# A four-layer graph network on one core: score rows of the last stage by one transpose, a store and a broadcast load, in place of eight transposes and two powers

## The chip, the cores and the metric

One core of one Trainium2 chip. The time is the device time of one execution in microseconds; a lower one is better. The profile is one further execution, taken by the hardware profiler.

## The reference

`x` is (16, 1024, 128), `adj` a 0/1 matrix (16, 1024, 1024). Four layers, each with a layer norm and a relu ahead of it and added to `x`. Layer 0 is a mean over neighbours with two batch norms. The others are attentions over each of the 16 graphs:

```python
# layer 1 ("A"); layer 3 ("C") is the same with adj > 0, other weights, and an elu on its result
Wh = h @ W.T
s, t = Wh @ a_src, Wh @ a_dst
e = leaky_relu(s[:, :, None] + t[:, None, :], 0.2)
alpha = softmax(where(adj == 0, -inf, e), axis=-1)
x = x + alpha @ Wh
# layer 2 ("B")
e = leaky_relu(einsum('bid,bjd,d->bij', h, h, a_0), 0.2)      # only adj == 1 occurs besides 0
x = x + softmax(where(adj == 1, e, -9e15), -1) @ h
```

For A and C the kernel splits the exponential: exp(leaky(s + t)) is, up to factors for a row or a column, the larger of a power of s (a row) and a power of t (a value for each partition). So a weight tile is `max(row_e, least) * mask`.

## The kernel before

Stage one (to about 285 us) reads `adj`, makes the masks and layer 0's means; stage two (to about 450 us) does layer 0's second product. The change is in the last stage, which runs from there to the end.

The last stage does layers A, B and C for all 16 graphs as one pipeline. In round `i` graph `i` is in A's product, graph `i - 1` in B, graph `i - 2` in C, and A's weights of graph `i + 1` are prepared. `run(i)` on each engine writes out its order by hand; nothing but semaphores joins the queues. `b` is a graph, `j` a tile of 128 rows of the adjacency (8 of them), `c` a tile of 128 results.

- **TensorE** (`run`, L1333): eight Gram tiles of B (`gram`, L1304, four matmuls of 512 columns and two halves each), between them C's turned input, values, highest score and rows; then A's product (`weigh`, L1319, eight times 8 tiles, the matmuls at L1329), then B's product and between its tiles A's preparation for the next graph (turned input, `values`, `highest`, `rows`), then C's product. A result tile `c` lies in one of two pairs of PSUM banks, changed every two tiles (`take(free_q, ...)`), so tile `c` waits until ScalarE has taken tiles `c - 4` and `c - 3` (for C's tile 2: B's last two tiles).
- **The rows** (`rows`, L1277): `us` holds 1,024 scores as 8 columns of 128 partitions. Each column is broadcast to 128x128 and transposed, four to a call, so that all 128 partitions of a PSUM bank (`LAST`) hold 512 scores. `row_power` (L1104) on ScalarE makes the power of each half into `row_e` (128x1024). Each half waits for the other through the one bank.
- **VectorE** (`run`, L924): the weight tiles of A and C (`weights`, L877, operation at L884) read `row_e`, `least` and a mask tile from a ring of four; B's leaky relu (`leaky`, L889); the norms' statistics; the reciprocal sums of each pair of result tiles (`shares`, L897, operations at L901 and L903), for which ScalarE then scales the pair (`scaled`, L1130, operation at L1141); `split_g`, `split_ag` and `complement` (L894), for which the next Gram product waits. In `run` the order around the A rows is: `weights("A", i + 1, 0)`, `lowest`, `weights("A", i + 1, 1)`, then `shares("B", i - 1, 3)`.
- **ScalarE** (`run`, L1153): copies of the Gram tiles, B's exponentials, norms, powers, scaled results.
- **SP** (L761) issues all loads and stores of the stage in order, each behind the semaphore that frees its buffer: an output, two mask pairs of A, two halves of `off` (B's mask), `qT`, mask pairs of C, `xA`, more masks.
- **GpSimd** makes only the powers for the norms (L819).

The first weight tile of a graph waits for both halves of the row:

```python
if j == 0:
    dve.wait_ge(S[x, "exp"], b + 1)
    dve.wait_ge(S[x, "s_row"], 2 * b + 2)
```

## Time and profile before

| | |
|---|---|
| median of 3 runs | 1610.05 us (1607.6 to 1613.08) |
| the profiled execution: its time, its span | 1606.74 us, 1604.9 us |
| TensorE busy | 1465.7 us, 91% |
| VectorE busy | 1137.0 us, 71% |
| ScalarE busy | 921.2 us, 57% |
| GpSimd busy | 203.2 us, 13% |
| score transposes (L1283) in the trace | 256 |
| DMA | 161.94 MB, 101 GB/s over the span |

Shares of busy time are averages over three stages with different limits. The rows further down are of the last stage; a row of the order of time gives the start from the span's start, the duration, engine, line, operation, what it writes and reads, how many alike stand together, and in brackets for how long the engine sat idle before it and for whom. Matmuls overlap: the distance between two starts says what one costs, not its own duration.

### The profile page before, as it was taken

To read this page: it belongs to the slowest core of one execution; us is meant where nothing else is said; L and a number is where in the kernel's file an instruction comes from. 1 tells how busy PE (TensorE), PEld (TensorE's weight loads), DVE (VectorE), ACT (ScalarE), POOL (GpSimd) and SP (SyncE) were. 2 spreads that over 40 slices of the span, in tenths; PEclk is the share of its full clock that TensorE was granted. 3 is DMA by queue.
4 is the path that set the end of the run, shared out by engine and by line. 5 is a ranking of instruction groups with operands and counts; after the bars stand their busy time and mean duration, and the time that the engine had idled before them with its cause. 6 is when DMAs were issued, how large, how long until landed. Compare 5 with 4: busy or idle time off the path is not lost. (4 is left out here: it accounts for less than half of the span.)

```text
span 1604.9 us, 32666 instructions
## 1 busy us (share of the span) xinstructions
PE 1465.7 (91%) x12740; PEld 1268.5 (79%) x12740; DVE 1137.0 (71%) x3198; ACT 921.2 (57%) x1825; POOL 203.2 (13%) x201
## 2 busy tenths in 40 slices
PE   3999998799836979999999999999999999999984
PEld 2999997555425859899898898988989889898774
DVE  3666664688635577887878878878788787886653
ACT  2777876122224666766657667566675766755620
POOL 4434430000000001011010111100111101010000
PEclk9999999799957989999999999999999999999996
DMA  9999991377811212213222132231322313212010
GB/s 189 207 209 213 210 210 67 110 244 244 288 39 47 79 47 69 76 47 99 54 85 81 39 106 76 57 93 28 112 74 54 93 35 105 67 34 61 28 35 25
DMA packets 108446, 161.94 MB, mean 101 GB/s; under 512 B 9344, under 2 KB 59136, under 8 KB 106240
## 3 DMA queue, kind: packets, MB, share of 16 engines
q1 hardware_dynamic: 85248, 117.86, 24.4%
q0 software_dynamic: 18432, 33.56, 11.4%
q10 hardware_dynamic: 4608, 8.39, 1.5%
q8 instruction: 102, 1.67, 0.4%
q14 instruction: 56, 0.46, 0.1%
HBM read 151.40 MB, written 41.94 MB: 120 GB/s over the span
## 5 line engine op out<-in xcount | busy, mean ns | idle before, releaser
L1329 PE MATMUL ps<-hV,wts_B 128*128 128x129 f32 x2048 | 246.2, 276 | 3.2 <-ACT wts_B L1128 3.0
L1329 PE MATMUL ps<-hP_A,wts_A 128*128 128x129 f32 x2048 | 239.0, 277 | 6.1 <-DVE wts_A L884 3.4
L1329 PE MATMUL ps<-hP_C,wts_C 128*128 128x129 f32 x2048 | 239.1, 277 | 6.0 <-DVE wts_C L884 6.0
L1329 PEld LDWEIGHTS ps<-hV,wts_B 128*128 128x128 f32 x2048 | 238.2, 192 | 4.6 <-ACT wts_B L1128 4.3
L1329 PEld LDWEIGHTS ps<-hP_A,wts_A 128*128 128x128 f32 x2048 | 234.4, 193 | 8.6 <-DVE wts_A L884 5.2
L1329 PEld LDWEIGHTS ps<-hP_C,wts_C 128*128 128x128 f32 x2048 | 234.3, 193 | 8.3 <-DVE wts_C L884 5.7
L889 DVE SCALAR_TENSOR_TENSOR wts_B<-wts_B 128x1024 f32<-128x1024 f32 x128 | 153.9, 1221 | 30.2 <-ACT wts_B L1124 30.2
L884 DVE SCALAR_TENSOR_TENSOR wts_A<-row_A,least_A,ring_A 128x1024 f32<-128x1024 f32 x128 | 161.2, 1275 | 9.2 <-ACT row_A L1108 8.3
L1124 ACT COPY wts_B<-ps 128x1024 f32<-128x1024 f32 x128 | 129.4, 1011 | 60.0 <-PE ps L1316 60.0
L884 DVE SCALAR_TENSOR_TENSOR wts_C<-row_C,least_C,ring_C 128x1024 f32<-128x1024 f32 x128 | 162.3, 1274 | 0.8 <-DMA ring_C<-maskT_scratch 0.8
L307 ACT ACTIVATE maskT<-ps 128x1024 fp8e4<-128x1024 bf16 x128 | 131.1, 1024 | 49.7 <-PE ps L341 37.7
L1128 ACT ACTIVATE wts_B<-wts_B,shiftB 128x1024 f32<-128x1024 f32 x128 | 141.9, 1153 | 0.0
L353 PE MATMUL ps<-x,adj_b 128*128 128x129 f16 x896 | 120.4, 223 | 18.4 <-DVE x L243 9.4
L354 PE MATMUL ps<-x,adj_b 128*128 128x128 f16 x896 | 120.7, 222 | 0.0
L1313 PE MATMUL ps<-g_hi,ag_hi 128*128 128x512 f16 x256 | 98.1, 383 | 14.7 <-DVE off L894 14.7
L353 PEld LDWEIGHTS ps<-x,adj_b 128*128 128x128 bf16 x896 | 88.2, 99 | 21.3 <-ACT whn L290 11.5
L1141 ACT ACTIVATE quo<-ps,rec_C 128x128 f32<-128x128 f32 x128 | 40.0, 363 | 112.9 <-DVE rec_C L903 112.9
L675 PE MATMUL ps<-maskT,row_hi 128*128 128x512 fp8e4 x256 | 97.3, 380 | 1.2 <-DVE row_lo L593 1.2
L1314 PE MATMUL ps<-g_lo,ag_hi 128*128 128x512 f16 x256 | 98.1, 383 | 0.0
L1315 PE MATMUL ps<-g_hi,ag_lo 128*128 128x512 f16 x256 | 98.1, 383 | 0.0
L1316 PE MATMUL ps<-off,pen_id 128*128 128x512 fp8e4 x256 | 97.9, 382 | 0.0
L675 PE MATMUL ps<-maskT,row_lo 128*128 128x512 fp8e4 x256 | 97.0, 379 | 0.0
(228 smaller groups left out, 2543.2 us busy)
## 6 DMA issues: line engine op xcount, KB each, us to landing
adj_b<-in_adj POOLq DMA_DIRECT2D x128, 256.0 KB, 9.1
maskT_scratch<-maskT SPq DMA_DIRECT2D x16, 1024.0 KB, 6.9
ring_A<-maskT_scratch SPq DMA_DIRECT2D x64, 256.0 KB, 3.3
off<-maskT_scratch SPq DMA_DIRECT2D x32, 512.0 KB, 6.7
ring_C<-maskT_scratch SPq DMA_DIRECT2D x64, 256.0 KB, 3.1
xa<-in_x SPq DMA_DIRECT2D x16, 512.0 KB, 4.3
whT_scratch<-whT_s ACTq DMA_DIRECT2D x32, 256.0 KB, 6.5
whT_b<-whT_scratch SPq DMA_DIRECT2D x16, 512.0 KB, 4.8
```

The source lines that it names most:

```text
L307: nc.scalar.activation(edges[:, b, c, :], psT[c % 2], ACT.Square, scale=EDGE_VALUE ** 0.5, saturate=False, accum_out=sq_all[:, n:n + 1]).t ...
L353: nc.tensor.matmul(q[:, 0:GW], adj_rc, h1, start=(r == 0), stop=False)
L354: nc.tensor.matmul(q[:, 0:P], adj_rc, h2, start=False, stop=False)
L675: last = nc.tensor.matmul(psP[par][:, c * HALF:(c + 1) * HALF], part[:, par, t, :], edges[:, b, t, c * HALF:(c + 1) * HALF], start=(t == 0 ...
L884: nc.vector.scalar_tensor_tensor(wts[x][:, j, :], row_e[x][:, :], least[x][:, j:j + 1], ring[x][:, j % MR, :], ALU.max, ALU.mult).then_inc ...
L889: nc.vector.scalar_tensor_tensor(wts["B"][:, j, :], wts["B"][:, j, :], SLOPE, wts["B"][:, j, :], ALU.mult, ALU.max).then_inc(S["B", "lrelu ...
L1124: nc.scalar.copy(wts["B"][:, j, :], P_SLOTS[j % 2]).then_inc(S["B", "kept"], 1)
L1128: nc.scalar.activation(wts["B"][:, j, :], wts["B"][:, j, :], ACT.Exp, bias=shiftB[:, 0:1]).then_inc(S["B", "exps"], 1)
L1313: nc.tensor.matmul(P_SLOTS[j % 2][:, cs], ag_hi[:, js], g_hi[:, cs], start=True, stop=False)
L1314: nc.tensor.matmul(P_SLOTS[j % 2][:, cs], ag_hi[:, js], g_lo[:, cs], start=False, stop=False)
L1315: nc.tensor.matmul(P_SLOTS[j % 2][:, cs], ag_lo[:, js], g_hi[:, cs], start=False, stop=False)
L1329: last = nc.tensor.matmul(Q_SLOTS[c // 2 % 2][:, c % 2, 0:PW], wts[x][:, j, c * P:c * P + P], src[:, j, :], start=(j == 0), stop=(j == T - 1))
```

## The change

The eight columns are turned by one transpose into 8 partitions of 128 (`rows`). ScalarE takes the power there, into `row_s`, 8x128, which lies in the unused `a_rep`; it waits for itself and issues a store of these 4 KB to `row_dram`, of which there are two for each layer. SP waits for the store's landing and issues a load that reads the 1,024 values once for each of the 128 partitions into `row_e` (512 KB into SBUF). The waits on `wts`, which kept the power from overwriting `row_e`, move to SP. The semaphore `s_row` now counts a DMA's 16. VectorE's queue is unchanged but for that count.

```diff
--- before.py
+++ after.py
@@ -103,6 +103,7 @@
         whT_dram = nc.dram_tensor("whT_scratch", (B, P, N), fp32).ap()
         maskT_dram = nc.dram_tensor("maskT_scratch", (B, P, T, N), u8).ap()
         pTf_dram = nc.dram_tensor("pTf_scratch", (B, P, N), fp32).ap()
+        row_dram = {x: nc.dram_tensor(f"row_scratch_{x}", (2, T, P), fp32).ap() for x in "AC"}
         NT = B * T
         RSCALE = 1024.0
         ROW_MAX = 6e4
@@ -703,6 +704,7 @@
             wts = {x: sbc(f"wts_{x}", [P, T, N]) for x in "ABC"}
 
             row_e = {x: sbc(f"row_{x}", [P, N]) for x in cases}
+            row_s = {x: a_rep[0:T, k, :] for k, x in enumerate(cases)}
             ring = {"A": ring_A, "C": sbc("ring_C", [P, MR, N], u8)}
             off_int, off_fp8 = off[:, :, :].bitcast(i32), off[:, :, :].bitcast(fp8)
             elu, quo = sbc("elu", [P, T, P]), sbc("quo", [P, T, P])
@@ -727,7 +729,7 @@
             S = {}
             for x in cases:
                 for n in ("var", "rstd", "shift", "h", "hT_made", "hT", "s_made", "s_row", "peak", "top_made", "top",
-                          "us", "te", "exp", "wh_made", "prod", "wts", "tile", "rec", "quo", "done"):
+                          "us", "te", "exp", "s_kept", "s_out", "wh_made", "prod", "wts", "tile", "rec", "quo", "done"):
                     S[x, n] = csem(f"{x}_{n}")
             S["A", "ring"], S["C", "ring"] = ring_A_in, [csem(f"C_ring{k}") for k in range(2)]
             for n in ("q", "qT_made", "x1"):
@@ -772,6 +774,14 @@
                             sp.wait_ge(S["B", "gram"], (b - 1) * T + 4 * h + 4)
                         sp.dma_start(off[:, 4 * h:4 * h + 4, :], maskT_dram[b, :, 4 * h:4 * h + 4, :]).then_inc(S["B", "ring"][h], 16)
 
+                    def load_row(x, b):
+
+                        sp.wait_ge(S[x, "s_out"], (b + 1) * 16)
+                        if b > 0:
+                            sp.wait_ge(S[x, "wts"], b * T)
+                        sp.dma_start(row_e[x][:, :], row_dram[x][b % 2].rearrange("t p -> (t p)").partition_broadcast(P)) \
+                            .then_inc(S[x, "s_row"], 16)
+
                     def load_q(b):
                         if b > 0:
                             sp.wait_ge(S["A", "qT_made"], b)
@@ -794,6 +804,9 @@
                             load_mask("A", i + 1, 1)
                         if 0 < i < B:
                             load_off(i, 0)
+                        if 0 <= i - 2 < B:
+                            load_row("C", i - 2)
+                        if 0 < i < B:
                             load_off(i, 1)
                         if 1 <= i + 2 < B:
                             load_q(i + 2)
@@ -802,6 +815,8 @@
                             load_mask("C", i - 2, 3)
                         if 2 <= i + 2 < B:
                             load_x(i + 2)
+                        if 0 <= i + 1 < B:
+                            load_row("A", i + 1)
                         if 0 <= i - 1 < B:
                             load_mask("C", i - 1, 0)
                             load_mask("C", i - 1, 1)
@@ -880,7 +895,7 @@
                             dve.wait_ge(S[x, "ring"][j // 2 % 2], (b * (PAIRS // 2) + j // 4 + 1) * 16)
                         if j == 0:
                             dve.wait_ge(S[x, "exp"], b + 1)
-                            dve.wait_ge(S[x, "s_row"], 2 * b + 2)
+                            dve.wait_ge(S[x, "s_row"], (b + 1) * 16)
                         nc.vector.scalar_tensor_tensor(wts[x][:, j, :], row_e[x][:, :], least[x][:, j:j + 1], ring[x][:, j % MR, :],
                                                        ALU.max, ALU.mult).then_inc(S[x, "wts"], 1)
 
@@ -1101,12 +1116,15 @@
                         nc.scalar.activation(hP[x][:, :, P:PW], te[x][:, :].unsqueeze(2), ACT.Exp)
                         nc.scalar.activation(least[x][:, :], te[x][:, :], ACT.Exp, scale=SLOPE - 1.0).then_inc(S[x, "exp"], 1)
 
-                    def row_power(x, b, h):
-                        act.wait_ge(S[x, "s_made"], 2 * b + h + 1)
-                        if h == 0 and b > 0:
-                            act.wait_ge(S[x, "wts"], b * T)
-                        nc.scalar.activation(row_e[x][:, h * HALF:(h + 1) * HALF], LAST[x], ACT.Exp, scale=1.0 - SLOPE) \
-                            .then_inc(S[x, "s_row"], 1)
+                    def row_power(x, b):
+                        act.wait_ge(S[x, "s_made"], b + 1)
+                        if b > 0:
+                            act.wait_ge(S[x, "s_out"], b * 16)
+                        nc.scalar.activation(row_s[x][:, :], LAST[x][0:T, 0:P], ACT.Exp, scale=1.0 - SLOPE).then_inc(S[x, "s_kept"], 1)
+                        act.wait_ge(S[x, "s_kept"], b + 1)
+                        if b > 1:
+                            act.wait_ge(S[x, "s_row"], (b - 1) * 16)
+                        act.dma_start(row_dram[x][b % 2], row_s[x][:, :]).then_inc(S[x, "s_out"], 16)
 
                     def factors(x, b, h):
 
@@ -1176,13 +1194,11 @@
                         if GW:
                             keep_scores(i - 1, 5)
                         if CA:
-                            row_power("C", i - 2, 0)
+                            row_power("C", i - 2)
                         if GW:
                             keep_scores(i - 1, 6)
                             score_exps(i - 1, 2)
                             keep_scores(i - 1, 7)
-                        if CA:
-                            row_power("C", i - 2, 1)
                         if GW:
                             for j in (3, 4, 5, 6):
                                 score_exps(i - 1, j)
@@ -1219,8 +1235,7 @@
                         if AA:
                             normed("B", i, newB, 1)
                         if nextA:
-                            row_power("A", i + 1, 0)
-                            row_power("A", i + 1, 1)
+                            row_power("A", i + 1)
                         if GW:
                             scaled("B", i - 1, 2)
                         if nextA:
@@ -1274,15 +1289,11 @@
                             last = nc.tensor.transpose(TURNS[x][:, t * P:t * P + P], src[:, t, 0:P], ident[:, :])
                         last.then_inc(S[x, "hT_made"], 1)
 
-                    def rows(x, b, free, h):
-
-                        take(free, 1, S[x, "s_row"], 2 * b + h + 1)
-                        if h == 0:
-                            pe.wait_ge(S[x, "us"], b + 1)
-                        for t in range(T // 2):
-                            last = nc.tensor.transpose(LAST[x][:, t * P:t * P + P],
-                                                       us[x][:, h * T // 2 + t:h * T // 2 + t + 1].to_broadcast([P, P]), ident[:, :])
-                        last.then_inc(S[x, "s_made"], 1)
+                    def rows(x, b, free):
+
+                        take(free, 1, S[x, "s_kept"], b + 1)
+                        pe.wait_ge(S[x, "us"], b + 1)
+                        nc.tensor.transpose(LAST[x][0:T, 0:P], us[x][:, :], ident[:, :]).then_inc(S[x, "s_made"], 1)
 
                     def highest(x, b, free, slot):
                         take(free, slot, S[x, "top"], b + 1)
@@ -1342,8 +1353,8 @@
                                     values("C", i - 2, free_q, (j - 2) * T // 2, (j - 1) * T // 2)
                                 if j == 4:
                                     highest("C", i - 2, free_q, 1)
-                                if j in (5, 7):
-                                    rows("C", i - 2, free_q, (j - 5) // 2)
+                                if j == 5:
+                                    rows("C", i - 2, free_q)
                         for c in range(T):
                             if AA:
                                 weigh("A", i, c)
@@ -1359,8 +1370,8 @@
                                     values("A", i + 1, free_p, 0, T)
                                 if c == 3:
                                     highest("A", i + 1, free_p, 1)
-                                if c in (4, 5):
-                                    rows("A", i + 1, free_p, c - 4)
+                                if c == 4:
+                                    rows("A", i + 1, free_p)
                         for c in range(T):
                             if CA:
                                 weigh("C", i - 2, c)
```

On TensorE, in a steady round around A's rows (`us_A` are the scores, `hV`, `wts_B` the operands of B's product). Before:

```order
L1329 MATMUL ps<-hV,wts_B 128x129 x8
L1290 MATMUL ps<-ident,peak_A 128x128
L1329 MATMUL ps<-hV,wts_B 128x129 x8
L1283 MATMUL ps<-ident,us_A 128x128 x4
L1329 MATMUL ps<-hV,wts_B 128x129 x8
L1283 MATMUL ps<-ident,us_A 128x128 x4
L1329 MATMUL ps<-hV,wts_B 128x129 x16
L1329 MATMUL ps<-hP_C,wts_C 128x129 x24
```

And with the change:

```order
L1340 MATMUL ps<-hV,wts_B 128x129 x8
L1301 MATMUL ps<-ident,peak_A 128x128
L1340 MATMUL ps<-hV,wts_B 128x129 x8
L1296 MATMUL ps<-ident,us_A 8x128
L1340 MATMUL ps<-hV,wts_B 128x129 x24
L1340 MATMUL ps<-hP_C,wts_C 128x129 x24
```

One transpose stands in the place of the first four; the second four are gone, and B's last three tiles follow each other.

On SP, one steady round with the change (`row_scratch` is the DRAM buffer):

```order
L797 DMA out<-xC 128x8x128
L769 DMA ring_A<-maskT_scratch 128x2048 x2
L775 DMA off<-maskT_scratch 128x4096
L782 DMA row_C<-row_scratch_C 128x1024
L775 DMA off<-maskT_scratch 128x4096
L788 DMA qT<-pTf_scratch 128x1024
L769 DMA ring_C<-maskT_scratch 128x2048 x2
L793 DMA xA<-in_x 128x8x128
L782 DMA row_A<-row_scratch_A 128x1024
L769 DMA ring_C<-maskT_scratch 128x2048 x2
L769 DMA ring_A<-maskT_scratch 128x2048 x2
```

The two row loads are new. C's stands between the halves of `off`, A's behind `xA` and ahead of two mask pairs each of C and of A; the rest keeps its order.

## Rows read from the trace of the kernel before

**Rows 1.** Stretch, us; busy us of PE, PEld, DVE, ACT, POOL; clock, DMA
```profile
943.74:961.68 17.94, 17.94 (x164) 17.94 (x162) 14.32 (x43) 10.04 (x26) 2.60 (x1) 1.00 0.29 70
```

**Rows 2.** TensorE in order of time in one steady round: start us, us
```profile
911.12 0.38 PE L1313 MATMUL ps<-g_hi,ag_hi 128*128 128x512 f16 x1
...
924.24 0.60 PE L1283 MATMUL ps<-ident,us_C 128*128 128x128 f32 x4
...
955.44 0.60 PE L1283 MATMUL ps<-ident,us_A 128*128 128x128 f32 x4
955.88 1.95 PE L1329 MATMUL ps<-hV,wts_B 128*128 128x129 f32 x16
...
961.68 5.52 PE L1329 MATMUL ps<-hP_C,wts_C 128*128 128x129 f32 x48
...
976.85 0.38 PE L1313 MATMUL ps<-g_hi,ag_hi 128*128 128x512 f16 x1
```

**Rows 3.** ScalarE in order of time, the same round
```profile
956.85 0.57 ACT L1108 ACTIVATE row_A<-ps 128x512 f32<-128x512 f32 x1
...
962.31 0.63 ACT L1141 ACTIVATE xC<-ps,rec_B 128x128 f32<-128x128 f32 x2 [1.86 <-DVE rec_B L903]
```

**Rows 4.** SP's queue in order of time, the same round and the last one
```profile
929.71 0.92 SPq L773 DMA_DIRECT2D off<-maskT_scratch  x2
...
1560.86 0.39 SPq L787 DMA_DIRECT2D out<-xC  x1
```

**Rows 5.** From issue to landing, by tile: whT_s, pT_b, whT_b; steady rounds: xA, off
```profile
DMA to landing us min/median/max: 2.0/6.5/8.2
...
DMA to landing us min/median/max: 2.9/2.9/10.4
...
DMA to landing us min/median/max: 3.2/4.8/5.6
...
DMA to landing us min/median/max: 4.2/4.5/6.3
...
DMA to landing us min/median/max: 5.6/6.9/8.2
```

**Rows 6.** VectorE in order of time, from this round and the one before
```profile
904.17 0.16 DVE L901 TENSOR_SCALAR rec_C<-ps 128x2 f32<-128x2 f32 x1 [1.13 <-PE ps L1329]
...
908.48 1.27 DVE L894 TENSOR_SCALAR off<-off 128x1024 int32<-128x1024 int32 x2
...
937.17 1.28 DVE L884 SCALAR_TENSOR_TENSOR wts_C<-row_C,least_C,ring_C 128x1024 f32<-128x1024 f32 x1
...
959.37 1.28 DVE L884 SCALAR_TENSOR_TENSOR wts_A<-row_A,least_A,ring_A 128x1024 f32<-128x1024 f32 x1
...
961.88 0.16 DVE L901 TENSOR_SCALAR rec_B<-ps 128x2 f32<-128x2 f32 x1
```

**Rows 7.** ScalarE, VectorE and TensorE in the first three rounds
```profile
467.81 0.60 ACT L1108 ACTIVATE row_A<-ps 128x512 f32<-128x512 f32 x1 [0.33 <-PE ps L1283]
...
470.35 1.28 DVE L884 SCALAR_TENSOR_TENSOR wts_A<-row_A,least_A,ring_A 128x1024 f32<-128x1024 f32 x1 [3.22 <-ACT row_A L1108]
...
519.75 0.59 PE L1313 MATMUL ps<-g_hi,ag_hi 128*128 128x512 f16 x1 [6.46 <-DVE off L894]
...
580.67 0.58 PE L1313 MATMUL ps<-g_hi,ag_hi 128*128 128x512 f16 x1 [8.24 <-DVE off L894]
```

**Rows 8.** VectorE in the last round
```profile
1560.75 4.87 DVE L884 SCALAR_TENSOR_TENSOR wts_C<-row_C,least_C,ring_C 128x1024 f32<-128x1024 f32 x4
```

**Rows 9.** TensorE after idle times, in order of time
```profile
500.29 2.02 PE L1299 MATMUL ps<-w_use,hT_c 128*128 128x130 f32 x16 [2.41 <-ACT hT_c L1094]
...
570.53 1.91 PE L1274 MATMUL ps<-ident,hV 128*128 128x128 f32 x8 [2.18 <-ACT hP_A L1116]
...
1518.82 0.49 PE L1329 MATMUL ps<-hV,wts_B 128*128 128x129 f32 x2 [1.75 <-ACT wts_B L1128]
...
1522.97 14.62 PE L1329 MATMUL ps<-hV,wts_B 128*128 128x129 f32 x114 [0.24 <-ACT wts_B L1128]
```

## The prediction

> **What bounds the kernel now.** I read the page's slices first, then the steady rounds of the last stage, then single queues. The last stage takes some 1,150 of the 1,604.9 us, and in the middle of it TensorE never idles: where the graph layers' B product runs it is busy for all of 17.94 us, VectorE for 14.32 and ScalarE for 10.04 [rows 1]. One round, from one Gram product to the next, lasts 976.85 - 911.12 = 65.73 us [rows 2]. So in a steady round a TensorE instruction taken away is time won, provided that nothing else becomes late. The question is what stands behind TensorE with little slack.
>
> **What is removed.** A group of four score transposes starts at 955.44, the next matmul at 955.88 [rows 2]: 0.44 us, 0.11 each. A round has four such groups, two for A and two for C. The change leaves one transpose for each layer (again 128 moving columns, so 0.11 us), and 14 of 16 go: 14 x 0.11 = 1.54 us a round, 0.77 in the Gram stretch (C), 0.77 in the B stretch (A). ScalarE loses two powers of 0.57 us or a little more for each layer [rows 3] and gets one over 128 columns (0.3 to 0.4 us; two of its operations on 128 columns take 0.62 [rows 3]) and a DMA issue, 0.39 us where SP makes one [rows 4]. That is no loss, and ScalarE isn't the bound; I count nothing for it.
>
> **What is added: a path through DRAM.** From the end of the power to a row on all partitions there are now two transfers in series, with SP between. The trace of before has neither.
> - The store of 4 KB. A store of 256 KB landed in 2.0 us at least, one of 512 KB in 2.9 [rows 5]; the line through both meets no bytes at 1.1. Bounds 1.1 and 2.0; I take 1.7, nearer to the measured row, as a landing has a part that doesn't shrink.
> - SP's wake-up, some 0.1 us.
> - The load of 512 KB in rows of 4 KB. As much from DRAM took 3.2 us at least and 4.8 at the median for whT_b, 4.2 at least for xA, and 5.6 to 8.2 for the off loads, which stand in a crowd [rows 5]. SP has nothing else in flight when A's row is fetched, so 3.6. That all 128 rows read the same 4 KB has no row; it is a rival below.
>
> Together 5.4 us (bounds 1.1 + 0.1 + 3.2 = 4.4 and 2.0 + 0.1 + 4.8 = 6.9). The Trainium skill (DMA: Bandwidth & Descriptors, Anatomy of one DMA) gives some 2.0 us fixed, most of it the receipt of the last write and heaviest at HBM, plus the bytes at 436 GB/s; by that estimate the two take 2.0 and 3.2 us, 5.3 with the wake-up, and the sum would be 1.7 us lower. Its Rules for kernel authors say that a transfer under 64 KB is mostly overhead, which speaks against the 4 KB store.
>
> **Layer A, the steady round.** ScalarE takes A's power at 956.85 [rows 3], right behind the second half of hV, which the change leaves. It ends at about 957.2, the store is issued at 957.25, and the row is there at 957.25 + 5.4 = 962.65. VectorE wants it at 959.37 [rows 6]: A's first weight tile starts 3.3 us late. Behind it in VectorE's queue stand the second tile and then the shares of B's last pair, now at 961.88 [rows 6]. ScalarE turns these into quotients from 962.31 on, for 0.62 us [rows 3], and only then is the second pair of PSUM banks free. TensorE needs these banks for C's third tile. C starts at 961.68, and its 48 matmuls of three tiles take 5.52 us with the last one's tail of 0.16 [rows 2]: 1.79 us a tile, so the third starts at 961.68 + 3.58 = 965.26. That is a slack of 965.26 - 962.93 = 2.3 us. With TensorE 0.77 us earlier it is 1.55, and the lateness is 3.3: **TensorE stalls 1.75 us**, more than the 1.54 that it has won in the whole round.
>
> It doesn't end there. VectorE's lateness runs on through C's stretch. Its largest idle time there, 1.13 us [rows 6], is spent beside GpSimd's power of C's variances, which starts later too, so I count only 0.15 us as recovered: 3.15 late. The first complement before the next Gram product then starts at 908.48 + 65.73 + 3.15 = 977.4 [rows 6], needs half of the two's 1.27, and lets the product begin at 978.1; TensorE itself is ready at 976.85 + 1.75 - 0.77 = 977.85 [rows 2]. So 0.25 us more. In the Gram stretch VectorE waits several times for TensorE and ScalarE, and is level again when it needs C's columns. The round: 1.75 + 0.25 - 1.54 = **+0.46**. Rows of A are made beside a C product in 13 rounds: **+6.0 us**. Each us of the path through DRAM is a us in each of them.
>
> **Layer C, the steady round.** C's scores are turned at 924.24 [rows 2], some 1 us later comes the power, and its 4 KB are there before 928. SP issues the last output, two A masks and the first off half before the row, which takes the place of the second off half, at about 930.2 [rows 4]. It stands in the crowd: off took 6.9 us at the median [rows 5], so 937.1. VectorE wants it at 937.17 less 0.77 [rows 6]; it waits 0.7 us, and TensorE doesn't need its next shares for 2 us more. Nothing; if the row lands over 2 us later, it begins to cost. The second off half and qT come about 2 us later and are needed over 5 us after that. The C masks that now stand behind A's row on SP are for the next round.
>
> **The ends.** Three rounds at the start hang on VectorE. In the first the power starts at 467.81 [rows 7]; now one transpose stands ahead of it in place of four, it is done at 467.9, the row lands at 473.3, and the tile that started at 470.35 [rows 7] is 3.0 us late. In the next two TensorE waits for the complement until 519.75 and 580.67 [rows 7], behind the same VectorE chain. The tiles start 3.3 us late, and some idle time in between is used up: +2.2 and +2.8. Sum **+8.0**. Two rounds near the end have C rows but no A row: 2 x 0.8, **-1.6**. In the last, everything waits for C's row: its first tile starts at 1560.75 [rows 8], and SP issues an output at 1560.86 [rows 4] ahead of the row, which goes out at 1561.3 and shares the rings (4.2 us): 1565.5, **+4.7**.
>
> **Sum**: 6.0 + 8.0 - 1.6 + 4.7 = +17 us. The profiled execution took 1,606.74, 3.3 under the median of the three runs; on the median that makes 1610 + 17 = **1627 us**, 1.1% slower. The path's length enters 13 + 3 + 1 = 17 times: its bounds of 4.4 and 6.9 us give 1610 and 1653. A difference under 0.3% (4.8 us) can't be told from none.
>
> **Rivals.**
> - *The path is shorter (faster).* It decides at 4.1 us: 17 x 1.3 = 22 less than my sum. Then the wait on VectorE is nearly inside the slack of 1.55 us and the removed transposes win. With a store of 1.1 and a load of 2.6, 3.8 in all: 17 - 27 = -10, 1600 us. For it: the rings are empty there. Against: no load of 512 KB took under 3.2 us. 0.10.
> - *It just cancels:* 4.4 to 4.7 us, the store at its lower bound and the load near the shortest row: 1610 to 1615. 0.14.
> - *The load is slow, since all 128 rows read the same 4 KB.* If it lands like a load in the crowd (6.9 us [rows 5]), the path is 8.7 us: 17 + 17 x 3.3 = +73, 1683; halfway, 1655. Against: nothing in the trace says that one address is slower. 0.12.
> - *The stall also lets TensorE's clock fall.* After 2.18 us of idle time eight transposes took 1.91 us (the 1.2 GHz level); after 2.41 us elsewhere 16 matmuls took 2.02 (2.4 GHz). After a wait of 1.75 us, in a product with short gaps, the 114 matmuls left took 14.62 us [rows 9], where 114 x 0.112 = 12.8: 1.8 us for one fall. If it fell in each of 13 rounds: +23, 1650; in half of them 1639. My stall stands among dense work, which neither row has. 0.18. The Trainium skill (TensorE: Matmul & The Clock Gate, Part 1) says that the throttled level is the default and that only activity lifts it.
> - *My case* as worked out, 1615 to 1640: 0.46.
>
> **How the numbers follow.** Faster by over 0.3%: the first rival, 0.10. Within 0.3%: 0.14. Slower: 0.46 + 0.12 + 0.18 = 0.76. The range reaches from 1608, just under what cancels, to 1660, beyond the falls of the clock and the halfway case of the slow load; about 0.1 is left out on either side.
>
> **What would show it.** Right: A's row landing 5 to 6 us after the store's issue; VectorE waiting some 3 us for a DMA before A's first tile in every round; a new idle time on TensorE of 1.5 to 2 us before C's third tile, released by ScalarE's B quotients; rounds of 66.2 us. Wrong: rounds of 64.2 us and TensorE without gaps (path under 4 us); a wait at C's first tile of over 2 us (the crowd costs after all); or matmuls at half clock behind each gap.

## The result, and the profile after

The changed kernel takes **1633.5 us** (median of 4 runs, 1630.9 to 1635.1), the kernel before beside it 1609.1 (4 runs): a ratio of 1.0148 with a 95% interval of 1.0131 to 1.0166, so 1.3 to 1.7% slower. The profiled execution took 1630.85 us with a span of 1629.1, against 1606.74 and 1604.9. Of all the runs further down one, of run 11, took 2577 us at a mean granted clock of 0.56, where its four others took 1599 to 1608; nothing here explains it, and the ratio there leaves it out.

The head of the page and some of its costliest groups, of the changed kernel:

```profile
PE 1450.7 (89%) x12516; PEld 1242.4 (76%) x12516; DVE 1133.0 (70%) x3198; ACT 891.4 (55%) x1793; POOL 203.2 (12%) x201
...
L1340 PE MATMUL ps<-hP_C,wts_C 128*128 128x129 f32 x2048 | 242.9, 278 | 32.5 <-ACT xC L1159 19.1
...
L899 DVE SCALAR_TENSOR_TENSOR wts_A<-row_A,least_A,ring_A 128x1024 f32<-128x1024 f32 x128 | 161.3, 1276 | 61.7 <-DMA row_A<-row_scratch_A 61.0
L899 DVE SCALAR_TENSOR_TENSOR wts_C<-row_C,least_C,ring_C 128x1024 f32<-128x1024 f32 x128 | 162.3, 1274 | 26.7 <-DMA row_C<-row_scratch_C 25.9
```

TensorE, VectorE and ScalarE are all busy for less time than before, by 15, 4 and 30 us, and the kernel is 24 us longer. The work went down and the waits went up: VectorE waits 61 us for A's rows and 26 for C's, and TensorE 19.1 for ScalarE in C's product.

TensorE in order of time, a steady round of the changed kernel (start us, us, in brackets the idle time before and who ended it):

```profile
923.98 0.38 PE L1324 MATMUL ps<-g_hi,ag_hi 128*128 128x512 f16 x1
...
927.43 1.04 PE L1289 MATMUL ps<-ident,hN 128*128 128x128 f32 x8
928.75 0.39 PE L1324 MATMUL ps<-g_hi,ag_hi 128*128 128x512 f16 x1 [0.28 <-ACT wts_B L1142]
...
930.67 1.13 PE L1310 MATMUL ps<-w_use,hT_c 128*128 128x130 f32 x8
...
941.38 1.95 PE L1340 MATMUL ps<-hP_A,wts_A 128*128 128x129 f32 x16
...
968.26 0.27 PE L1296 MATMUL ps<-ident,us_A 128*8 128x128 f32 x1
968.37 5.52 PE L1340 MATMUL ps<-hV,wts_B 128*128 128x129 f32 x48
973.73 3.74 PE L1340 MATMUL ps<-hP_C,wts_C 128*128 128x129 f32 x32
978.99 2.05 PE L1340 MATMUL ps<-hP_C,wts_C 128*128 128x129 f32 x16 [1.52 <-ACT xC L1159]
980.87 1.04 PE L1289 MATMUL ps<-ident,hV 128*128 128x128 f32 x8
981.75 9.10 PE L1340 MATMUL ps<-hP_C,wts_C 128*128 128x129 f32 x80
```

Read it against [rows 2]. The 48 matmuls that opened C's product in one piece are now cut after two tiles: the third starts at 978.99, where 973.73 + 3.58 = 977.31 was due. The one score transpose costs 968.37 - 968.26 = 0.11 us. The stretches, from start to start (the Gram stretch reaches from the first Gram matmul to A's product):

| us, steady round | before | changed |
|---|---|---|
| Gram product, C's turn beside it | 17.45 | 17.40 |
| A's and B's products | 33.11 | 32.35 |
| C's product | 15.17 | 17.12 |
| round | 65.73 | 66.87 |

C's seven removed transposes should have made the Gram stretch 0.77 us shorter; it is 0.05 shorter, so 0.72 us were added in it. C's product is 1.95 us longer.

The path of A's row, on ScalarE, on SP's queue and on VectorE, same round:

```profile
969.65 0.25 ACT L1123 ACTIVATE a_rep<-ps 8x128 f32<-8x128 f32 x1
969.93 0.27 ACTq L1127 DMA_DIRECT2D row_scratch_A<-a_rep  x1
...
978.31 0.62 ACT L1159 ACTIVATE xC<-ps,rec_B 128x128 f32<-128x128 f32 x2 [5.87 <-DVE rec_B L918]
```
```profile
971.15 0.32 SPq L782 DMA_DIRECT2D row_A<-row_scratch_A  x1
```
```profile
975.40 1.29 DVE L899 SCALAR_TENSOR_TENSOR wts_A<-row_A,least_A,ring_A 128x1024 f32<-128x1024 f32 x1 [3.47 <-DMA row_A<-row_scratch_A]
976.61 0.17 DVE L880 TENSOR_TENSOR rec_top<-rec_top,least_A 128x8 f32<-128x8 f32 x1
976.68 1.28 DVE L899 SCALAR_TENSOR_TENSOR wts_A<-row_A,least_A,ring_A 128x1024 f32<-128x1024 f32 x1
977.88 0.15 DVE L916 TENSOR_SCALAR rec_B<-ps 128x2 f32<-128x2 f32 x1
```

From the store's issue to the first weight tile: 975.40 - 969.93 = 5.47 us, 1.22 for the store and SP's answer, 4.25 for the load. VectorE stands for 3.47 us with nothing else to do; B's last sums wait behind two tiles until 977.88; ScalarE's quotients, 5.87 us idle, start at 978.31; then the banks are free and TensorE goes on.

VectorE's lateness goes on behind that. At the next Gram product (start 923.98, in the kernel before 911.12) VectorE and ScalarE of the changed kernel:

```profile
923.16 1.27 DVE L909 TENSOR_SCALAR off<-off 128x1024 int32<-128x1024 int32 x2
...
926.97 0.17 DVE L918 RECIPROCAL rec_C<-rec_C 128x2 f32<-128x2 f32 x1
927.16 0.63 ACT L1159 ACTIVATE quo<-ps,rec_C 128x128 f32<-128x128 f32 x2 [1.73 <-DVE rec_C L918]
927.68 1.93 ACT L1142 COPY wts_B<-ps 128x1024 f32<-128x1024 f32 x2
```

And of the kernel before:

```profile
912.28 0.17 DVE L903 RECIPROCAL rec_C<-rec_C 128x2 f32<-128x2 f32 x1
912.48 0.62 ACT L1141 ACTIVATE quo<-ps,rec_C 128x128 f32<-128x128 f32 x2 [1.73 <-DVE rec_C L903]
913.04 1.01 ACT L1124 COPY wts_B<-ps 128x1024 f32<-128x1024 f32 x1
```

The first copy of B's scores starts 1.92 us after the Gram product's start in the kernel before, and 3.70 us after it in the changed one; TensorE waits for it at 928.75.

Over the 13 steady rounds (waits by engine and line, from 640 to 1480 us: us in total, times, longest):

```profile
DVE wts_A L899 <- DMA row_A<-row_scratch_A: 44.5, 13, 3.7
...
PE ps L1340 <- ACT xC L1159: 19.1, 13, 1.7
DVE wts_C L899 <- DMA row_C<-row_scratch_C: 17.6, 12, 2.3
...
PE ps L1324 <- ACT wts_B L1142: 4.0, 13, 0.6
```

Where the span's 24.2 us lie: 1.6 us before the stage's first score transpose (468.71 against 467.15), where the change hasn't touched anything yet; 6.1 between there and the second Gram product; 13.0 in the 13 rounds after it; nothing in the last round but one; 3.5 from the last Gram product to the end.

### The profile page after: what moved, and what is told of

The parts are those of the page before. It is cut to its first block and busy times, and to the rows that moved or that the text cites. A ratio compares the mean times of both kernels' runs of the same rounds, so it can differ in the third digit from the quotient of the medians.

```text
span 1629.1 us, 32308 instructions
## 1 busy us (share of the span) xinstructions
PE 1450.7 (89%) x12516; PEld 1242.4 (76%) x12516; DVE 1133.0 (70%) x3198; ACT 891.4 (55%) x1793; POOL 203.2 (12%) x201
## 5 line engine op out<-in xcount | busy, mean ns | idle before, releaser
L1340 PE MATMUL ps<-hP_C,wts_C 128*128 128x129 f32 x2048 | 242.9, 278 | 32.5 <-ACT xC L1159 19.1
L1340 PE MATMUL ps<-hV,wts_B 128*128 128x129 f32 x2048 | 242.2, 275 | 3.7 <-ACT wts_B L1146 3.6
L308 ACT ACTIVATE maskT<-ps 128x1024 fp8e4<-128x1024 bf16 x128 | 131.1, 1024 | 50.6 <-PE ps L342 39.1
L354 PE MATMUL ps<-x,adj_b 128*128 128x129 f16 x896 | 120.1, 222 | 19.1 <-ACT whn L291 9.7
L1159 ACT ACTIVATE xC<-ps,rec_B 128x128 f32<-128x128 f32 x128 | 39.9, 363 | 139.6 <-DVE rec_B L918 139.6
```

Source lines behind the costliest of these rows:

```text
L308: nc.scalar.activation(edges[:, b, c, :], psT[c % 2], ACT.Square, scale=EDGE_VALUE ** 0.5, saturate=False, accum_out=sq_all[:, n:n + 1]).t ...
L354: nc.tensor.matmul(q[:, 0:GW], adj_rc, h1, start=(r == 0), stop=False)
L1340: last = nc.tensor.matmul(Q_SLOTS[c // 2 % 2][:, c % 2, 0:PW], wts[x][:, j, c * P:c * P + P], src[:, j, :], start=(j == 0), stop=(j == T - 1))
```

## Experiments

Each was timed beside the kernel before on one chip (its median there 1608.5 to 1610.0). Differences between runs are differences of medians. Round lengths are from one Gram product to the next in its trace.

**1. C's row alone through DRAM, A's by transposes.** A helper says which rows keep the old path:

```diff
+            def direct(x, b):
+                return x == "A"
```

> A's row is made by the sixteen transposes of the kernel before, C's row goes through DRAM. Theory (only A's row is late; C's has time to spare): 0.77 us leave each Gram stretch of some 14 rounds, minus 11, and in the last round C's row has nothing to hide its path, plus 4.7: about 1603 us, 1600 to 1606, against 1609 of the kernel before, with no wait of TensorE before C's third tile. Rival 1 (the added 0.7 us of the Gram stretch comes from C's own row, by its transfers or its place in ScalarE's queue): 1609 to 1614, and the Gram stretch stays at 17.4 us. Rival 2 (each row through DRAM costs the same): about 1621.

Measured: **1602.7 us** (ratio 0.9964, 0.9951 to 0.9978). Stretches of this kernel, C's product and then the Gram product (stretch, us; busy us of PE, PEld, DVE, ACT, POOL; clock, DMA share, GB/s):

```profile
958.05:973.22 15.17, 15.17 (x138) 15.16 (x137) 13.24 (x38) 8.62 (x22) 2.60 (x1) 1.00 0.14 39
973.22:989.91 16.69, 16.69 (x92) 9.44 (x90) 13.70 (x22) 12.33 (x17) 0.00 (x0) 1.00 0.00 1
```

TensorE is without gaps in both, and the round is 64.97 us, 0.76 less. VectorE still waits 16.9 us for C's row in all, and that costs nothing. C's half of the change is a gain, and the 0.72 us that the changed kernel adds in the Gram stretch isn't its doing: here that stretch is 16.69 us, the full 0.76 shorter.

**2. A's row alone through DRAM** (`return x == "C"`).

> C's row is made by the sixteen transposes of the kernel before, A's row goes through DRAM. Theory (A's row carries the whole loss, and C's half of the change was a gain): a steady round is 1.9 us longer than before (C's stretch 1.95 more, B's and A's 0.77 less, the Gram stretch 0.72 more), 13 times 25, the first rounds 8, the last nothing: about 1643 us, 1638 to 1648, above the changed kernel's 1633. Rival (each row costs the same): about 1621. Rival (the two rows' loads hinder each other, so that one alone is cheap): below 1621.

Measured: **1639.0 us** (1.0181, 1.0168 to 1.0195), above the whole change, with rounds of 67.1 to 67.9 us; TensorE waits 19.3 us for B's quotients in 13 rounds. So the loss is A's, and C's half takes some off. Against the kernel before, the two halves alone come to 29.2 - 7.0 = +22.2 us, and both together to +24.4: the two rows hardly hinder each other.

**3. B's last sums ahead of A's first tiles**, VectorE:

```diff
+                        if GW:
+                            shares("B", i - 1, 3)
                         if nextA:
                             weights("A", i + 1, 0)
                             lowest("A")
                             weights("A", i + 1, 1)
-                        if GW:
-                            shares("B", i - 1, 3)
```

> The changed kernel, with VectorE taking B's last sums of weights ahead of A's first two weight tiles instead of behind them. Theory (TensorE's wait before C's third tile is VectorE standing at A's row with B's sums behind it): the wait of 1.5 to 1.75 us is gone from 13 rounds, 20 to 23 us less than 1633, so 1610 to 1614; VectorE still waits some 3 us for A's row. Rival 1 (the lateness of VectorE comes back at C's later tiles, whose sums are still behind A's weight tiles): half of it, about 1622 to 1626. Rival 2 (the wait is the transfers' doing, not the order's): 1630 to 1635.

Measured: **1628.8 us** (1.0124, 1.0108 to 1.0139): 4.6 less, where I expected 20. TensorE's and VectorE's waits in this kernel, from 640 to 1480 us:

```profile
DVE wts_A L899 <- DMA row_A<-row_scratch_A: 13.5, 13, 1.6
PE ps L1324 <- DVE off L909: 13.4, 13, 1.1
...
PE ps L1324 <- ACT wts_B L1142: 4.1, 13, 0.6
```

The wait at C's third tile is gone from the list, so its cause was the order. But 1.03 us a round now stand where they weren't, at the start of the Gram product, for the masks' complements on VectorE (`off`). The first tile of A still starts at the row's landing, everything behind it is as late as before, and TensorE, 1.5 us earlier, meets that lateness one consumer further on. Rival 1 had the mechanism and the wrong place; the gain was under a quarter, not a half. One more expectation missed: VectorE waits 1.0 us a round for A's row, not 3, as it now waits first for the matmuls of B's last tiles.

**4. C's last quotients behind the first score copy**, ScalarE:

```diff
+                        if GW:
+                            keep_scores(i - 1, 0)
                         if post:
                             scaled("C", i - 3, 3)
                         if GW:
-                            keep_scores(i - 1, 0)
                             keep_scores(i - 1, 1)
```

> The changed kernel, with ScalarE's last quotients of C placed behind the first copy of B's scores instead of ahead of it. Theory (the Gram stretch is 0.7 us longer than it should be because the first score copies stand in ScalarE's queue behind quotients that a late VectorE holds back): 0.6 to 0.7 us less in 13 rounds, about 1624 to 1626 us, with the Gram stretch at 16.7 to 16.9 us and the wait before C's third tile unchanged. Rival 1 (TensorE's pace there is set by the values' turn, which comes as late as before): no change, 1631 to 1635. Rival 2 (the time left goes straight into a longer wait at C's third tile, since VectorE's round is what repeats): no change either, but with the Gram stretch shorter and C's stretch longer by the same amount.

Measured: **1623.9 us** (1.0092, 1.0076 to 1.0107), 9.6 less than the changed kernel. The Gram stretch is 1003.60 - 986.91 = 16.69 us, which is 17.45 less the 0.77 of the transposes, and the wait at C's third tile is still 18.1 us in 13 rounds. ScalarE in this kernel at the start of a Gram product:

```profile
988.84 1.01 ACT L1142 COPY wts_B<-ps 128x1024 f32<-128x1024 f32 x1 [0.47 <-PE ps L1328]
990.10 0.63 ACT L1159 ACTIVATE quo<-ps,rec_C 128x128 f32<-128x128 f32 x2 [0.25 <-DVE rec_C L918]
```

The copy now waits for TensorE alone, and the quotients for VectorE behind it. Both rivals are out: these 0.7 us a round were a wait that hangs on the order of ScalarE's queue.

**5. Both, and the complements too.** VectorE's order in C's product and on:

```diff
-W(A,0) lowest(A) W(A,1) shares(B,3) W(A,2) sum(B) stats(C,0) shares(C,0) stats(C,1)
-moments(C) W(A,3) shares(C,1) shifts(C) split W(A,4) shares(C,2) complements W(A,5) W(A,6) shares(C,3)
+shares(B,3) sum(B) stats(C,0) W(A,0) lowest(A) shares(C,0) stats(C,1) moments(C)
+W(A,1) W(A,2) shares(C,1) shifts(C) split W(A,3) shares(C,2) complements W(A,4) W(A,5) shares(C,3) W(A,6)
```

(W is `weights`, sum is `highest_share` and `add`, split is `split_g` and `split_ag`.) ScalarE is as in run 4.

> The changed kernel with VectorE's part of C's stretch in another order: B's last sums, sum B's second half, C's first statistics ahead of A's weight tiles, the complements of the masks ahead of A's fifth tile, and A's seventh tile at the start of the next round behind C's last sums; ScalarE's last quotients of C behind the first score copy, as in the run before. Theory (what is lost is only what waits behind the late row in VectorE's queue): neither C's third tile, nor the complements, nor the score copies wait; a steady round falls from 66.8 to 64.3 to 64.8 us, the removed transposes being a gain at last; 13 times 2.0 to 2.5 from 1633, or 1601 to 1607 us. Rival (VectorE's work after the row is too much for any order, so that the wait only moves once more): 1615 to 1625.

Measured: **1595.8 us** (0.9913, 0.9899 to 0.9927), 37.7 us less than the changed kernel and 14 less than the one before. VectorE in this kernel where A's row is wanted, and the stretch of C's product:

```profile
958.72 0.16 DVE L916 TENSOR_SCALAR rec_B<-ps 128x2 f32<-128x2 f32 x1 [1.99 <-PE ps L1337]
...
960.59 0.88 DVE L848 BATCH_NORM_STATS2 st_C<-xC 128x6 f32<-128x128 f32 x4
961.38 1.27 DVE L899 SCALAR_TENSOR_TENSOR wts_A<-row_A,least_A,ring_A 128x1024 f32<-128x1024 f32 x1
```
```profile
958.52:973.69 15.17, 15.17 (x139) 15.16 (x137) 13.54 (x38) 8.30 (x22) 2.60 (x1) 1.00 0.24 71
```

A's first tile no longer waits for a DMA. The store is issued at 954.72 in this round; by an estimate with the path of 5.47 us the row is there at 960.2, 1.2 us ahead of the tile. The round is 64.20 us (two of the 13 took 64.9), which is 65.73 less 1.53: all of the removed transposes' time, and nothing else. The time is below my 1601 to 1607, since the first rounds got most of their loss back too: from A's first product to the third Gram product 175.9 us go by, as before (175.9), where the changed kernel needs 181.6. Ahead of A's first product the row's path still costs its time: counted from the first score transpose it is 183.1 us, against 181.0 before and 188.3 in the changed kernel.

**6. The new order without the change.** The same two reorderings in the kernel before.

> The kernel before, transposes and all, with the same new orders on VectorE and ScalarE as in the run above. Theory (the order mends only what the late row spoils): within 4 us of the kernel before, 1605 to 1611, with rounds of 65.4 to 65.8 us. Rival (the order is a gain of its own, and the row's path is still a loss with it): 1590 to 1600, below the changed kernel with this order.

Measured: **1609.6 us** (1.0002, 0.9993 to 1.0011), rounds of 65.73. The order is worth nothing by itself. So the 14 us of run 5 are the change's, and the order only makes room for it. This trace also says how much chance lies ahead of the stage: its first score transpose starts at 471.75, 4.6 us later than in the kernel before, with no edit ahead of it.

**7. Transposes again at the ends**: `direct` is true for A's rows 0 to 2 and C's last row, in the old order.

> The changed kernel, with the sixteen transposes back for A's row in the first three rounds and for C's row in the last one. Theory (where the pipeline is not full the path has nothing to hide it): the 6.1 us that the first rounds take more than before and the 3.5 of the last come back, 1633 less 9 to 10: 1622 to 1626 us. Rival (the first rounds' loss is the same lateness of VectorE that a full round then takes over, and only moves into it): 1628 to 1631.

Measured: **1621.9 us** (1.0081, 1.0067 to 1.0094), 11.6 less. From the last Gram product to the end of the span it is 106.1 us, as before, against 109.6. The ends' terms were real. The medians give 11.6 us for the 9 to 10 that I expected, the spans of the two traces 9.9 (1619.2 against 1629.1).

**8. Different addresses for the 128 rows**:

```diff
-row_dram[x][b % 2].rearrange("t p -> (t p)").partition_broadcast(P)
+whT_dram[b]
```

> The changed kernel, with each partition's 4 KB of the row read from an address of its own (128 different rows of another DRAM tensor) instead of all from the same 4 KB; the weights and the output are therefore not those of the reference. Theory (the landing time is that of a load of 512 KB): row A still lands 3.9 to 4.2 us after its issue, and the time is that of the changed kernel, 1629 to 1637. Rival (reading one address 128 times is slow): the landing falls to 3 us or less and the time by 0.8 or more times 13, to 1620 or less. Opposite rival (the repeated address is quick and different ones are slower): landing above 4.6 us, the time above 1640.

Measured: 1630.5 us in one run. A's row from its issue to its landing, in the changed kernel and with different addresses (min, median, max of the steady rounds):

```profile
DMA to landing us min/median/max: 3.7/4.0/4.2
```
```profile
DMA to landing us min/median/max: 3.3/3.6/4.3
```

Reading one 4 KB row 128 times took 0.4 us longer than reading 128 rows, a tenth. My three theories had all set their bounds round this value: landing at 3.6 is between them. TensorE's wait at C's third tile is 14.2 us in 13 rounds here, against 19.1: 0.38 less a round, so these 0.4 us are paid in full. As an explanation of the loss the rival is out (rounds of 66.0 to 66.8 us still); as an effect it seems to be there, small, on the evidence of one execution. The rows read here had also been written long before, in stage one, so the address alone isn't shown to be the cause.

**9. Run 5 with transposes for C's last row**, the best version.

> The reordered kernel through DRAM (the run that took 1595.8 us), with the sixteen transposes back for C's row in the last round alone. Theory: the 3.5 to 4 us that the last round takes more with C's row through DRAM come back and nothing else moves: 1591.5 to 1593.5 us, 17 us below the kernel before. Rival (a late finish of the last round is hidden behind the output's transfers): 1594.5 to 1597.

Measured: **1590.8 us** (0.9891, 0.9875 to 0.9907), 17.6 us below the kernel before. That is 4.9 us less than run 5 by the medians, and 3.4 less by what each has on the kernel beside it (17.6 and 14.2), so about what I expected, 0.7 us under my range in the time itself. From the last Gram product to the end of the span it is 105.3 us against 110.1 in run 5.

**10 and 11. A longer path in the old and in the new order.** A's 4 KB are copied once more within DRAM ahead of the load:

```diff
+sp.dma_start(hop_dram[b % 2], source).then_inc(S[x, "s_hop"], 16)
+sp.wait_ge(S[x, "s_hop"], (b + 1) * 16)
```

> The changed kernel with A's row copied once more within DRAM ahead of its load (4 KB, waited for by SyncE), so that the row lands some 2 us later; C's row as it was. Theory (in this order each microsecond that the row is late goes into the round whole, its cover being used up): steady rounds of 68.6 to 69.1 us, 13 times 2 and 3 first rounds by 2, about 1661 to 1668 us. Rival (a wait that TensorE has anyway takes half of it): 1645 to 1652.

> The same longer path for A's row, in the reordered kernel (1595.8 us without it). Theory (the new order gives the row a place where VectorE has other work for 2 us more, or idle time behind it to catch up in): steady rounds stay within 0.3 us of 64.2, at most 4 us come from the first rounds, 1596 to 1601 us. Rival (the new order has only just enough slack): rounds of 65 to 66 us, 1606 to 1620 us.

Measured, old order: **1675.1 us** (1.0443, 1.0403 to 1.0483; four runs from 1669 to 1687), 42 us more, and above my 1661 to 1668. New order: **1602.1 us** (0.9966, 0.9939 to 0.9993), 6 more and 1 above my range. Of these, 5 are there by the third Gram product (657.2 against 652.0 us), of which 1.5 lie ahead of the stage's first score transpose (470.39 against 468.94), where the two kernels are alike. The steady rounds are 64.20 as without the hop, though VectorE now waits for A's row, 7.9 us in 13 rounds: it catches up. The hop itself takes 2.1 us, from its issue to the load's (median landing 1.9).

In the old order the wait at C's third tile grew from 1.5 to 3.3 us (39.6 over 12 rounds), by 1.8, but the round by 2.6, from 66.74 to 69.36 (means). The rest is in what follows the wait. Two rounds of this kernel, TensorE in order of time:

```profile
996.75 3.61 PE L1346 MATMUL ps<-hP_C,wts_C 128*128 128x129 f32 x16 [3.57 <-ACT xC L1165]
...
1066.72 2.05 PE L1346 MATMUL ps<-hP_C,wts_C 128*128 128x129 f32 x16 [3.48 <-ACT xC L1165]
```

And the same two places with their granted clock (stretch, us; busy us of PE, PEld, DVE, ACT, POOL; clock, DMA share, GB/s):

```profile
996.75:1001.07 4.32, 4.32 (x25) 4.32 (x26) 3.92 (x22) 1.61 (x6) 0.00 (x0) 0.62 0.23 58
1066.72:1069.48 2.76, 2.76 (x24) 2.76 (x25) 2.50 (x11) 1.11 (x5) 0.00 (x0) 1.00 0.35 94
```

Behind a wait of 3.57 us the granted clock was 0.62 of full, mostly the 1.2 GHz level, and 16 matmuls took 3.61 us; behind one of 3.48 it stayed at 2.4 GHz and they took 2.05. In 8 of the 12 rounds they took more than 2.6 us, and in a ninth 2.49 with a granted clock of 0.67 over the next 4.3 us; behind the other three, of 2.93, 3.48 and 3.48 us, the clock stayed at its full level. The three rounds without a fall took 68.0 to 68.5 us, the nine with one 68.9 to 70.6. So without a fall the longer path costs about 1.5 us a round, and a fall adds about 1.4. After the waits of 1.06 to 1.71 us in the changed kernel the 16 matmuls took 2.05 all 13 times.

## Why the prediction was right, and where it was not

The forecast of 1627 us, 1.1% slower, was 6 us short; the measured 1633.5 is inside the range, and the likeliest case was the one that came. Point by point:

- **The removed transposes, 1.54 us a round: right.** 0.76 less in A's and B's stretch, 0.76 less with C's half alone (run 1), 1.53 less with all waits gone (run 5).
- **The path, 5.4 us: right as a sum** (5.47), and that is luck, as two errors cancel: store and wake-up 1.22 for 1.8, load to first tile 4.25 for 3.6. I had said that nothing else is in flight beside the load; SP issues two C masks of 256 KB 0.4 us behind it, and how much of the 4.25 is theirs isn't shown. The Trainium skill (DMA: Bandwidth & Descriptors, Anatomy of one DMA) has some 2.0 us fixed for a transfer, as a fit to transfers that GpSimd issues; this 4 KB store, issued by ScalarE, was answered within 1.22 us, so for it the trace doesn't agree. For the load its estimate of 3.2 was 0.8 below the median landing of 4.0.
- **The stall at C's third tile, 1.75 us: right**, in place, chain and nearly in size. By starts it was 978.99 - 977.31 = 1.68 in the round shown; the idle times listed, which leave out the tail of the matmul before, are 1.52 there and 1.5 in the mean.
- **Behind it, +0.25: about right.** 0.16 at the complements, and 0.09 in which the third tile's matmuls take longer than before (1.88 us from start to start for 1.79), which I had not counted. That the 0.16 are a wait for the complements is read from distances: the Gram product starts 0.82 us after the first of them (923.16 to 923.98), the same as in run 3 (922.81 to 923.63), where the trace names the wait. My own sum was rounded up: 977.36 + 0.64 = 978.0 against 977.83 is 0.17, not 0.25.
- **"In the Gram stretch VectorE ... is level again": the step that failed.** Up to there 1.68 + 0.25 - 1.54 = +0.4 a round, as forecast. The missing 0.72 is in the Gram stretch. I had followed VectorE's lateness to the complements and then asked only what VectorE waits for, not who waits for VectorE: its last sums of C come 2.99 us after the Gram product's start (926.97, in the kernel before 1.16), ScalarE's quotients wait for them, and behind these in ScalarE's queue stand the copies that empty TensorE's score banks. Run 4 took that away and got 9.6 us back. With it the round shown is +1.14, and all 13 together are +13.0 in place of +6.0: 7 us, about what the forecast was short of. The other misses cancel: -1.9 in the first rounds, +0.4 at the end, +1.6 ahead of the first score transpose.
- **C's row: right.** It lands 7.5 us after its issue (I had 6.9), VectorE waits 1.3 us a round (2.3 at most), and nobody waits for VectorE there. So my sign of being wrong, a wait of over 2 us at C's first tile, came up at least once, and without a cost.
- **The ends.** First rounds +6.1 for +8.0; the last round but one 0 for -0.8, as the Gram stretch's wait ate the gain (17.41 us against 17.46); the last one +3.5 for 4.7 - 0.8 = +3.9. Its tile started 4.7 us late, as forecast: 20.7 us of shift on 1560.75 [rows 8] make 1581.5, and it started at 1586.2. Here too two errors cancel: the load went out at 1580.9, 1.1 us earlier than forecast (1561.3 + 20.7 = 1582.0), and took 5.3 us for 4.2.
- **"Each us of the path is a us in each of them": right as far as it went, and too low further on.** Run 8 shows it for 0.4 us less. Run 10 shows it further on: 1.8 us more wait, 2.6 more round, because the clock fell behind 9 of 12 waits of about 3 us.
- **The rivals.** Shorter path and cancelling: no, 5.47 us. One address: 0.4 us by run 8, not 3.3. Falling clock: not at waits up to 1.7 us, but it was the right worry, as run 10 shows; I had priced it from rows of another surrounding, and said so.

What I had not seen at all is that the loss hangs on the order and not on the path alone. What I had written held it: VectorE's queue has the tile that needs the row ahead of B's last sums and of the complements, for which others wait, while A's tiles themselves are wanted only in the next round's product.

**Still open.** The 1.6 us ahead of the first score transpose, which starts anywhere from 467.2 to 471.8 us in seven of the traces, so that chance can make them. The first rounds' loss in the old order mostly goes with either cure (runs 5 and 7), but wasn't split by place. Whether the load of A's row is faster with the two C masks held back wasn't tried.

## What to carry to other kernels

A transfer with a latency that nothing shortens may replace work of the engine that bounds the kernel, if what waits for it stands last in its own engine's queue. Before costing such a change as a loss, look at the waiting instruction's neighbours: those behind it that others wait for can go ahead of it, if its own result isn't wanted soon. Here that turned +24 us into -14 in the time, and with it 2.1 us more latency cost nothing in a steady round, where in the old order they cost 2.6. Curing the wait that the profile shows first isn't enough (run 3 got 5 of 20 us): list all consumers behind the late instruction, on the other engines' queues too, as each becomes the next wait. And at the ends, where nothing covers the latency, keep the old path.

## What the runs showed of the hardware

- A 4 KB store from 8 partitions to DRAM was answered by the next queue's issue in 1.22 us, and a 4 KB copy from DRAM to DRAM landed in 1.9 us (median). I had the first at 1.7 with the wake-up apart.
- 512 KB read from one 4 KB row to all partitions: 4.0 us (median) where only two loads of 256 KB were issued behind it, 7.5 in the crowd; from 128 rows 3.6 (one execution).
- TensorE's granted clock held through a wait of 1.7 us in dense matmul work each time, and fell behind 9 of 12 waits of 2.9 to 3.6 us (granted 0.50 to 0.67 over the next 4.3 us); two waits of 3.5 us came out differently. That the throttled level is the default and activity lifts it, as the Trainium skill has it (TensorE: Matmul & The Clock Gate, Part 1), agrees with the falls; it doesn't tell these two apart.
